# First attention of a two-layer cross-attention block: heads scored in pairs and weighted in fours, one masked maximum, and the context read batch by batch

## The reference

```
x = layer_norm(hidden_states, ln1_w, ln1_b)
q = (x @ q_w + q_b).reshape(B, LQ, H, HD).transpose(0, 2, 1, 3)      # H = 16, HD = 32
k = (encoder_hidden_states @ k_w + k_b).reshape(B, LK, H, HD).transpose(0, 2, 1, 3)
v = (encoder_hidden_states @ v_w + v_b).reshape(B, LK, H, HD).transpose(0, 2, 1, 3)
scores = jnp.einsum('bhqd,bhkd->bhqk', q, k) * scale
scores = jnp.where(mask, scores, mask_value)                          # mask_value: lowest float32
attn = jax.nn.softmax(scores, axis=-1)
out = jnp.einsum('bhqk,bhkd->bhqd', attn, v)
```

## Time and profile before

| what | value |
|---|---|
| median of 3 runs (lowest, highest) | 2629.13 us (2624.97, 2636.66) |
| span of the profiled execution, first to last instruction | 2629.4 us |
| PE busy | 2532.7 us, 96% |
| DVE, ACT, POOL busy | 44%, 41%, 21% |
| chain of waits, share on PE | 89% |
| DMA over the span | 129.99 MB, mean 49 GB/s |

### The profile page before, as it was taken

One profiled execution on the slowest core, in us unless ns is written; L12 is line 12 of the kernel. 1 busy time (PEld: TensorE's weight loads), 2 busy tenths in 40 slices (PEclk: granted clock), 3 DMA queues, 4 the chain that ended last, 5 costly groups with the idle time before them and its releaser, 6 DMA issues.

```text
span 2629.4 us, 45592 instructions
## 1 busy us (share of the span) xinstructions
PE 2532.7 (96%) x14242; PEld 2240.0 (85%) x14242; DVE 1153.7 (44%) x2353; ACT 1077.7 (41%) x2583; POOL 563.9 (21%) x775
## 2 busy tenths in 40 slices
PE   5999999898999999999999989999999999999899
PEld 4777777797989899899899769898998998997798
DVE  6666666546123333333433461334333334334643
ACT  3444444323344444444444333444444444443331
POOL 4001101323111222222211240122222122212331
PEclk9999999898999999999999989999999999999899
DMA  6200001111510110100111425001001002114120
GB/s 177 76 4 8 4 4 37 43 42 48 162 45 21 34 41 21 53 14 21 57 32 32 143 69 157 26 20 48 20 21 53 21 21 61 32 30 151 37 64 29
DMA packets 187337, 129.99 MB, mean 49 GB/s; under 512 B 52654, under 2 KB 183138, under 8 KB 187234
## 3 DMA queue, kind: packets, MB, share of 16 engines
q1 hardware_dynamic: 187234, 128.68, 16.5%
HBM read 95.60 MB, written 33.05 MB: 49 GB/s over the span
## 4 chain that ended last, share of the span: by engine, by line
PE 89%; issue 4%; DVE 3%; ACT 1%; POOL 1%; DMA 1%; SPq 0%; POOLq 0%; ACTq 0%; DVEq 0%
PE ps_v L1052 10%; PE ps_v L1053 9%; PE ps_v L1054 9%; PE ps_k L1052 9%; PE ps_o L1151 9%; PE ps_k L1054 9%; PE ps_k L1053 9%; PE ps_s L1052 5%; PE ps_s L1054 4%; PE ps_s L1053 4%; PE ps_t L1136 4%; PE ps_o L1052 3%; PE ps_o L1053 3%; PE ps_o L1054 3%; DVE act_t_lo L842 1%
## 5 line engine op out<-in xcount | busy, mean ns | idle before, releaser
L876 DVE SCALAR_TENSOR_TENSOR k_lo<-ps_k,col_b,k_hi 128x375 fp32r<-128x375 f32 x256 | 155.6, 608 | 675.1 <-ACT k_hi L646 675.1
L523 POOL TENSOR_TENSOR cs_lo<-ctx_t,cs_hi 128x1504 fp32r<-128x1504 f32 x72 | 249.3, 3464 | 761.9 <-DVE cs_hi L855 761.9
L1052 PE MATMUL ps_v<-w_b_hi,cs_hi 128*128 128x512 f32 (+1 forms) x928 | 392.8, 423 | 10.2 <-POOL w_b_lo L509 7.8
L1052 PE MATMUL ps_k<-cs_hi,w_a_hi 128*128 128x376 f32 x1152 | 389.5, 338 | 5.2 <-DVE k_lo L876 5.2
L1054 PE MATMUL ps_k<-cs_hi,w_a_lo 128*128 128x376 f32 x1152 | 385.6, 335 | 0.0
L1053 PE MATMUL ps_k<-cs_lo,w_a_hi 128*128 128x376 f32 x1152 | 385.1, 334 | 0.0
L1054 PE MATMUL ps_v<-w_b_hi,cs_lo 128*128 128x512 f32 (+1 forms) x928 | 366.0, 394 | 0.0
L1053 PE MATMUL ps_v<-w_b_lo,cs_hi 128*128 128x512 f32 (+1 forms) x928 | 365.9, 394 | 0.0
L646 ACT ACTIVATE k_hi<-ps_k,col_b 128x375 fp32r<-128x375 f32 x256 | 146.7, 573 | 424.3 <-PE ps_k L1054 424.3
L1151 PE MATMUL ps_o<-prob_t,v 128*128 128x112 f32 (+3 forms) x2304 | 310.1, 271 | 0.0
L1151 PEld LDWEIGHTS ps_o<-prob_t,v 128*128 128x128 f32 (+3 forms) x2304 | 276.3, 165 | 32.6 <-ACT prob_t L664 19.6
(11 more groups left out here) (173 smaller groups left out, 4438.2 us busy)
## 6 DMA issues: line engine op xcount, KB each, us to landing
w_raw_a<-in_blocks_a SPq DMA_DIRECT2D x104, 256.0 KB, 3.2
w_raw_b<-in_blocks_b SPq DMA_DIRECT2D x104, 256.0 KB, 3.3
q_lo<-q_scratch SPq DMA_DIRECT2D x72, 224.0 KB, 2.5
o_scratch<-o SPq DMA_DIRECT2D x64, 224.0 KB, 2.0
q_scratch<-prob SPq DMA_DIRECT2D x36, 224.0 KB, 2.5
q_scratch<-o SPq DMA_DIRECT2D x36, 224.0 KB, 2.5
cs_hi<-o_scratch SPq DMA_DIRECT2D x6, 672.0 KB, 4.2
cs_lo<-o_scratch SPq DMA_DIRECT2D x6, 672.0 KB, 4.3
```

The costliest lines, as they stand in the source:

```text
L523: pool.tensor_tensor(cs[place.parity][1][:, 0:DT * KW].rearrange("p (k n) -> p k n", k=DT), ctx_t[:, :, ds(place.b * KW, KW)], cs[place.pa ...
L876: dve.scalar_tensor_tensor(out=k[t % 2][1][:, 0:n], in0=ps_k[:, 0:n], scalar=cols(att)[:, ds(place.column((C_BK0, C_BK1), t), 1)], in1=k[t ...
L1052: pe.matmul(out, w_h, m_h, start=first, stop=False)
```

## The change

**Scores.** `score_pair` computes two heads at once: six matmuls in the order hi*hi of both heads, hi*lo of both, lo*hi of both. The heads lie on different 32 partitions and write different banks. It stands in the slots j = 0 and 2 for heads j and j + 1 of the next tile, and waits until both maxima of the pair before are taken.

**Weighted sums.** `weighted` runs once per tile, in slot j = 3 ahead of the turn, over all four heads: for each of three pieces of keys, the four heads after one another, each to its own 32 rows of `ps_o`. `prob_t` has four buffers.

**Mask and maximum.** `masked_maximum` puts the cap, the maximum and its negation in one `tensor_tensor_reduce`: (score + 0 or the lowest float) times -1, with the row minimum as a second result. The exponential takes scale -1. The mask of a batch takes one DVE instruction, not two.

**Output.** DVE adds the output's bias in the first attention, in slot j = 3 behind the maximum of that slot, and ACT does no longer.

**Context.** `ctx_t` gives way to two buffers `ctx_raw` of one batch. SP loads a batch's context (752 KB) at the head of the batch two before it, in all three attentions (72 loads), once the lo part of the batch of the same parity is made.

```diff
             def load_context(place):
+                wait(sp, cs_lo, place.batch - 1)
+                sp.dma_start(ctx_raw[place.parity][:],
+                             ctx_in[ds(place.b, 1)].rearrange("o p f -> (o p) f")).then_inc(ctx_in_sem[place.parity], 16)
...
                     if after:
                         load_q(after)
+                    if place.after(2):
+                        load_context(place.after(2))
...
             def context_lo(place):
                 pool.wait_ge(cs_hi, place.batch + 1)
-                pool.tensor_tensor(cs[place.parity][1][:, 0:DT * KW].rearrange("p (k n) -> p k n", k=DT),
-                                   ctx_t[:, :, ds(place.b * KW, KW)],
-                                   cs[place.parity][0][:, 0:DT * KW].rearrange("p (k n) -> p k n", k=DT),
-                                   ALU.subtract).then_inc(cs_lo, 1)
+                pool.tensor_tensor(cs[place.parity][1][:, 0:DT * KW], ctx_raw[place.parity][:],
+                                   cs[place.parity][0][:, 0:DT * KW], ALU.subtract).then_inc(cs_lo, 1)
...
             def context_hi(place):
+                dve.wait_ge(ctx_in_sem[place.parity], 16 * place.same_parity + 16)
+                dve.tensor_copy(cs[place.parity][0][:, 0:DT * KW], ctx_raw[place.parity][:]).then_inc(cs_hi, 1)
...
+                def mask_keys(place):
+                    dve.tensor_scalar(key_add[:], mask_u8[:, ds(place.b * LK, LK)], -1.0, LARGEST,
+                                      ALU.add, ALU.mult).then_inc(key_masked, 1)
+                    dve.wait_ge(key_masked, place.batch + 1)
+
+                def masked_maximum(place, t, j):
                     unit = place.unit + sub * t + j
                     if (t, j) == (0, 0):
+                        mask_keys(place)
                     dve.wait_ge(s_mm, unit + 1)
                     wait(dve, t_mm, unit - SUB0 + 1)
-                    dve.tensor_tensor(prob_0[j][0:LQ, 0:LK], ps_s[j % 2][0:LQ, 0:LK], key_cap[:], ALU.min).then_inc(s_cap, 1)
+                    dve.tensor_tensor_reduce(out=prob_0[j][0:LQ, 0:LK], in0=ps_s[j % 2][0:LQ, 0:LK], in1=key_add[:],
+                                             scale=-1.0, scalar=LARGEST, op0=ALU.add, op1=ALU.min,
+                                             accum_out=max_neg[0:LQ, j:j + 1]).then_inc(s_max, 1)
...
+                def output(place, t):
+                    dve.wait_ge(av_mm, place.tile + t + 1)
...
+                    dve.tensor_scalar(o[place.parity][:, t * LQ:(t + 1) * LQ], ps_o[t % 2][:, 0:LQ],
+                                      col_a[:, ds(place.column((C_BV0, C_BV1), t), 1)], None, ALU.add).then_inc(o_ev, 1)
...
+                def score_pair(place, t, j):
+                    unit = place.unit + sub * t + j
                     if j == 0:
                         pe.wait_ge(k_lo, place.tile + t + 1)
...
+                    wait(pe, s_max, unit)
+                    for i, (q_s, k_s) in enumerate(((0, 0), (0, 1), (1, 0))):
+                        for head in (j, j + 1):
+                            rows = slice(HD0 * head, HD0 * (head + 1))
+                            last = pe.matmul(ps_s[head % 2][0:LQ, 0:KW], q[place.parity][q_s][rows, t * LQ:(t + 1) * LQ],
+                                             k[t % 2][k_s][rows, :], start=(i == 0), stop=(i == 2))
+                            if i == 2:
+                                last.then_inc(s_mm, 1)
...
+                def weighted(place, t):
...
+                    wait(pe, o_ev, NT * place.batch + t - 1)
+                    pe.wait_ge(t_ev, place.unit + sub * (t + 1))
                     for i, n in enumerate(att.vals()):
+                        for j in range(sub):
+                            rows = slice(0, P) if layer else slice(HD0 * j, HD0 * (j + 1))
+                            last = pe.matmul(ps_o[t % 2][rows, 0:LQ],
+                                             v[place.parity][0:n, i, t * P + rows.start:t * P + rows.stop],
+                                             turned_to(layer, t, j)[0:n, i * LQ:(i + 1) * LQ], start=(i == 0), stop=(i == 2))
                     last.then_inc(av_mm, 1)
...
                             if j in att.key_parts and place.key(t + att.key_ahead):
                                 key(*place.key(t + att.key_ahead), att.key_parts[j])
+                            if layer == 0 and j == sub - 1:
+                                weighted(place, t)
                             if place.at(t, j, 1):
                                 turn(*place.at(t, j, 1))
+                            ahead = place.at(t, j, att.score_ahead)
+                            if ahead and layer == 0 and j % 2 == 0:
+                                score_pair(*ahead)
```

More of the change, by code:

```diff
@@ L194, in sem @@
             return ctx.enter_context(nc.semaphore(name))
-        ctx_t = sb("ctx_t", [P, DT, NB * KW])
+        ctx_raw = [sb(f"ctx_raw{i}", [P, DT * KW]) for i in range(2)]
         x = sb("x", [P, RT, D])
@@ L346, in softmax_buffers, with turned_to @@
             return (t % 2, prob[t % 2]) if layer else (j, prob_0[j])
+        def turned_to(layer, t, j):
+            return prob_t[t % 2] if layer else prob_t[j]
         def staged(i):
@@ L389, in contexts @@
                     load_block(0, 1)
+                    return
+                for parity in range(2):
+                    load_context(Place(att, a, 0, 0, parity))
             def query(layer, a, group, slot, n, step):
@@ L662, in turned @@
                     act.wait_ge(t_mm, unit + 1)
-                    wait(act, av_mm, unit - 1)
-                    act.activation(prob_t[buf][:], ps_t[buf][:, 0:3 * LQ], ACT.Identity).then_inc(t_ev, 1)
+                    wait(act, av_mm, place.tile + t if layer == 0 else place.tile + t - 1)
+                    act.activation(turned_to(layer, t, j)[:], ps_t[buf][:, 0:3 * LQ], ACT.Identity).then_inc(t_ev, 1)
                 def exp(place, t, j):
@@ L1138, in turn @@
                     last.then_inc(t_mm, 1)
-                def weighted(place, t, j):
-                    unit, buf = place.unit + sub * t + j, (j if layer == 0 else t) % 2
-                    if (t, j) == (0, 0):
+                def weighted(place, t):
+                    if t == 0:
                         pe.wait_ge(v_ev, 3 * place.batch + 3)
@@ L1167, in prologue @@
                     value(place, 2)
-                    scores(place, 0, 0)
-                    if layer == 1:
+                    if layer == 0:
+                        for j in range(0, SUB0, 2):
+                            score_pair(place, 0, j)
+                    else:
+                        scores(place, 0, 0)
                         key(place, 2)
-                    for unit in range(1, att.score_ahead):
-                        scores(*place.at(0, 0, unit))
+                        scores(place, 1, 0)
                     turn(place, 0, 0)
```

114 lines of the change are left out of this document (44 added, 70 removed).

## The result

| | median, us | runs | lowest to highest |
|---|---|---|---|
| before | 2631.94 | 4 | 2624.97 to 2636.66 |
| after | 2559.39 | 4 | 2551.53 to 2563.27 |

The ratio is 0.9727, with a 95% interval of 0.9704 to 0.9750: 2.7% faster. The forecast was 2564 (2536 to 2602). The profiled execution after has a span of 2561.3 us, 68.1 less than before. It is the longest of its kernel's four executions (its granted clock was 0.973; the shortest had 0.978), so a comparison of two single profiles can be off by some us.

A forecast was written before the change was run, and what follows sets the result against it. PE's own instructions were taken to bound the attentions. The terms, 44.8 + 59.5 - 3 - 6 + 1 - 29 - 2 = 65 us off the profiled 2629.4, gave 2564 us, range 2536 to 2602.

The forecast's parts named there:

- Pairs: First attention's scores: a pair of heads costs what one unit costs, so 64 pairs save 44.8 us.
- rival (e): First attention's scores: pairs don't run side by side although the order changed; costs 45 us, 2609; chance 0.03.
- Weighted sums: First attention: four heads' sums take 0.90 us per tile, saving 1.86 on each of 32 tiles, 59.5 us.
- (b): Weighted sums: column groups don't overlap, twelve matmuls take 2.4 us per tile; 2600 us; chance 0.08.
- (f): Weighted sums: groups overlap but matmuls aren't fed fast enough, 1.5 us per tile, 19 us lost; 2583; chance 0.09.
- Second pair waits for the maximum: First attention: PE newly waits 0.3 to 0.4 us per batch for head 1's maximum, 3 us in all.
- (c): Fused maximum on DVE takes 1.25 us, so DVE's chain sets the first attention's time; 2590; chance 0.12.
- Blocked scaling: DVE's scaling behind the context's hi part loses to POOL's subtraction in six batches, 6.1 us each; 29 us more.
- (a): DVE's scaling still starts ahead of POOL's subtraction in the loop's four batches; 22 us less, 2542; chance 0.17.
- Last batch: First attention's last batch: DVE sets the pace, 23.9 us after 29.5, saving 5.6 instead of 11.6; 6 us back.
- Streaming: Context loaded per batch: hidden in the second layer, except 1 us at each of its attentions' entries, 2 in all.
- Rival (d): Context loads land late in the second layer; at 14 us, 64 batches lose 1.5 each, 2660; chance 0.03.

The follow-up runs named there:

- e1: Changed kernel with each head's scores taken alone again instead of in pairs; first attention 50.9 us longer than the changed kernel's.
- e9: Changed kernel with a semaphore instruction ahead of POOL's context subtraction and that subtraction in four pieces; 3.7% faster than the kernel before, attention 30.5 us shorter than the changed kernel's.
- e5: Changed kernel with the fused maximum split into two DVE instructions, mask add and row maximum; attention 20.2 us longer than the changed kernel's.
- e4: Kernel before with only the context streamed through two rotating buffers; 17 us longer than the kernel before, 11.9 of it in the first attention.
- e8: Changed kernel with one semaphore instruction on POOL between its wait and the context subtraction; attention 23.4 us shorter than the changed kernel's.
- e11: Kernel before with the context streamed and a semaphore instruction between POOL's wait and its subtraction; ratio 1.0003 to the kernel before, attention 5.9 us shorter.
- e3: Changed kernel with POOL's context subtraction issued in four pieces of 376 columns; attention 22.2 us shorter than the changed kernel's, median 28 us lower.
- e6: Changed kernel with each head's weighted sums taken alone again, scores still in pairs; attention 46.0 us longer than the changed kernel's.
- e2: Changed kernel with a tile's twelve weighted-sum matmuls issued head by head, not key tile by key tile; attention 24.4 us longer than the changed kernel's.
- e7: Changed kernel with a score pair's six matmuls issued head by head, not turn about; ratio 0.9728 to the kernel before, against the changed kernel's 0.9727.

## Why the prediction was right, point by point

The mechanisms of the main terms held, and the span fell by 68.1 us where the sum had 65. That it came so close is in part luck: terms that were 16 us too low and others that were 13 us too high cancelled.

- **Pairs**: right, 0.70 for two, so rival (e) falls. Taken out alone they are worth 1.6 per tile and not 1.4, since the turn next to them changes too (e1).
- **Weighted sums**: taken as 0.90, measured 0.71, the low bound within 0.02. Rivals (b) and (f) fall: 24 issues in 0.71 us are 30 ns each. The Trainium skill's 62 ns per matmul for a stream decoded the slower way ("TensorE: Matmul & The Clock Gate", Part 1, on the spacing of matmuls) doesn't bind here.
- **Pairs and sums together**: forecast 3.26 us per tile. Where no race is lost, a batch takes 46.75 us before and 32.86 in e9, 3.47 per tile. Over the 28 tiles with a value product that is 6 us more than forecast, and the 0.19 of the sums is most of it.
- **Second pair waits for the maximum**, 3 us: wrong for the changed kernel. No such wait stands in its list for 118 to 340 us. It appeared only in e5, with the maximum 0.47 us longer; (c) is therefore refuted for the fused form. For the unfused one its size came (20.2 us) but not its sign, a wait in every tile: the first tile of a batch stayed at 8.5 us.
- **Blocked scaling**: the race is lost in all six batches, as forecast, with the 3.1 us idle as forecast, and (a) fell because POOL's wait is now inside its instruction, which e4, e8 and e11 show. Mis-sized was the rest: 30.5 us for six (after less e9) is 5.1 each, not 6.1. In the loop it is 3.46 us in the blocked tile (11.69 against 8.23) and 1.15 in the next (9.86 against 8.71): next to the idle time there is about 1.5 for the clock and the wait behind, where I had put 3.0. In batches 0 and 1 it is 6.2 and 5.7. What differs is the clock: over the 10 us that hold the slow stretch its mean is 0.66 in batches 0 and 1 (105 to 115 and 143 to 153 us) and 0.83 in the loop (180 to 190), 3.4 and 1.7 us lost, where I had put 2.6 for each; and the 0.4 us of the second pair is in no list of waits. The kernel before had lost 7.5. Net 23 in place of 29.
- **Last batch**: the step that failed. I had added up instructions, 29.5 before and 23.9 after, DVE as the bound, and so 5.6 us of gain. From the start of tile 28's last sums to that of tile 32's it took 30.9 us before (411.50 to 442.42, the last six of the x12) and 30.6 after (340.89 to 371.50), a gain of 0.3:

```profile
411.50 0.76 PE L1151 MATMUL ps_o<-prob_t,v 128*32 128x112 f32 x6
...
441.81 1.38 PE L1151 MATMUL ps_o<-prob_t,v 128*32 128x112 f32 x12
```

```profile
340.89 0.78 PE L1155 MATMUL ps_o<-prob_t,v 128*32 128x112 f32 x24
...
371.50 1.35 PE L1155 MATMUL ps_o<-prob_t,v 128*32 128x112 f32 x24 [0.63 <-ACT prob_t L659]
```

  The windows of the kernel before, then of the changed one:

```profile
421.00:431.00 10.00, 10.00 (x67) 7.78 (x66) 7.80 (x20) 5.94 (x18) 0.00 (x0) 1.00 0.10 28
431.00:441.00 10.00, 9.49 (x67) 6.73 (x66) 9.04 (x24) 6.93 (x20) 0.00 (x0) 1.00 0.09 26
```

```profile
348.00:356.00 8.00, 7.39 (x60) 6.15 (x60) 5.89 (x19) 4.67 (x15) 2.39 (x2) 0.79 0.12 35
356.00:364.00 8.00, 5.66 (x48) 3.93 (x48) 5.94 (x21) 5.66 (x17) 0.00 (x0) 0.69 0.12 34
364.00:372.00 8.00, 4.80 (x50) 3.76 (x52) 3.52 (x13) 4.15 (x13) 0.00 (x0) 0.50 0.12 34
```

  DVE isn't full (5.94 of 8). With the shorter PE work nothing covers the round from scores over maximum, exponential and scaling back to the turn; PE stops several times, and its granted clock falls from 1.00 to means of 0.79, 0.69 and 0.50 (the lower level, 1.2 GHz), which lengthens the work that is left. 5.3 us of the forecast's gain went there. The runs show a part of what is round and what is clock: from tile 29's sums to tile 30's the changed kernel, e9, e8 and e3 run the same code, and take 8.35, 8.38, 9.43 and 9.58 us at mean clocks of 0.80, 0.80, 0.64 and 0.64. So 3.4 us more at the lower level cost 1.1 us. The whole stretch of 30.6 us has a mean of 0.74, 16 us at the lower level; at the same rate that is an estimate of 5 us, most of what the last batch took beyond the forecast's 23.9. In the later tiles, where PE stands longer, the rate wasn't measured.
- **Start**: the scores start 3.0 us later, where the sum had nothing; the 14 starts spread over 7 us, so one profile can't show a term of this size. From the first scores to the first tile's sums it takes 13.0 us in place of 15.6; what is left for it of the forecast, when 27 tiles, the waits, the races and the last batch are taken out, is 5.4 of gain, the first maxima's 1 us included. Its mean clock was 0.74 where it had been 0.89, which is up to 1.7 us of the difference.
- **Streaming**: hidden in the second layer, as forecast. Rival (d) falls: a load of 752 KB lands after 4.4 us in the median and 7.5 at most, and DVE waits for one only at the two entries. There PE waited 0.65 us at most; all that lies behind the attention grew by 0.7 us, within its spread, against 2 forecast. DVE did wait, 11.66 and 1.31 us at the first entry, and SP, which issued stores of q at 593.26, issued the next load of weights only at 603.78:

```profile
597.73 0.94 DVE L844 CAST cs_hi<-ctx_raw 128x1504 fp32r<-128x1504 f32 x1 [11.66 <-DMA ctx_raw<-in_ctx_t]
599.99 3.00 DVE L844 CAST cs_hi<-ctx_raw 128x1504 fp32r<-128x1504 f32 x1 [1.31 <-DMA ctx_raw<-in_ctx_t]
```

By size: +6 (tiles), +3 (no wait for the maximum), +6 (races), +1 (behind the attention), -5 (last batch), -3 (the later start), -3 (up to the first sums), -2 (from the last sums to the projection, 6.3 to 8.4 us). That takes 65 to 68, with 68.1 measured; each of the small terms is read from one profile of each kernel.

## What to carry to other kernels

When a kernel's main engine gets shorter work, look again at every wait that it covered: here 0.02 us between POOL and DVE decided 4.6 to 6.2 us per batch, and one idle instruction or a split of the long operation gave back 22 to 23 us of the attention, both together 30. Look at the granted clock beside every difference too: up to 12 us in e1, and as many in e6, came from the clock and not from the part that was taken out. Price a matmul that is taken out with its neighbours' changeover, and a stage without filler work by the round over all engines, not by the busiest one. Four heads' sums on separate column groups cost what one head's do if they are issued in turn (0.71 us); issued one group after another they cost about twice that (1.36).

## What the runs showed of the hardware that I had not expected

- Matmuls on different column groups start out of program order, in 5 to 7 ns behind each other, but only about two groups deep: 24 issues in 0.71 us interleaved, 1.36 in sequence (e2). For two row groups the order makes no difference (e7).
- A group of three transposes holds PE for 0.39 us ahead of the scores and 0.23 ahead of the value product.
- POOL's float32 subtraction and DVE's float32 scaling exclude each other for the whole instruction, also when POOL's is in four pieces (1.17 us behind the first of four pieces that start 0.95 to 1.06 us apart, e3); DVE's fused maximum, which reads PSUM, isn't held (0.54 us beside POOL, e8). Who starts first goes first: POOL 0.03 us ahead in the changed kernel, DVE 0.07 to 0.08 us ahead in e8.
- In the last batch of the attention PE's granted clock stays at the lower level (0.50) through 8 us in which PE is busy 60% of the time.
